# Second home for x of odd groups, batch sums of group 3 on the vector engine, and weight-pair sums two steps ahead

## The reference

```python
# x (32, 64, 512), cond (32, 256)
q_emb = relu(cond @ W3 + b3)
v_sum = sum(x, axis=1, keepdims=True)          # over the 64 tokens of a batch
x1 = (n * x + v_sum) * q_emb[:, None, :]       # n = 64
h0 = relu(x1 @ W2 + b2)
w1, w2 = ternary(W_fc), ternary(W_proj)        # per 64 weights: scale = mean |w|, w -> round(w / scale) in -1, 0, 1, times scale
h = square(relu(h0 @ w1.T))                    # 2048 hidden units
hn = h * rsqrt(mean(square(h)) + eps)
out = x + hn @ w2.T
```

## Time and profile before

| | us |
|---|---|
| median of 3 runs | 320.93 (320.6 to 321.79) |
| the profiled execution | 321.12 |
| its span | 319.1 |
| PE busy | 313.4 (98%), 1326 records |
| DVE busy | 210.6 (66%) |
| ACT busy | 192.1 (60%) |
| POOL busy | 113.0 (35%) |
| granted TensorE clock | 0.998 |

### The profile page before, as it was taken

One profiled execution on the slowest core, in us unless ns is written; L12 is line 12 of the kernel. 1 busy time (PEld: TensorE's weight loads), 2 busy tenths in 40 slices (PEclk: granted clock), 3 DMA queues, 4 the chain that ended last, 5 costly groups with the idle time before them and its releaser, 6 DMA issues.

```text
span 319.1 us, 3835 instructions
## 1 busy us (share of the span) xinstructions
PE 313.4 (98%) x1326; PEld 238.8 (75%) x1326; DVE 210.6 (66%) x290; ACT 192.1 (60%) x282; POOL 113.0 (35%) x94
## 2 busy tenths in 40 slices
PE   8999999999999999999999999999999999999995
PEld 7664746545888788888888888888888888888884
DVE  0539989788888846676556655755655675665555
ACT  1658988799996884455544454644455554445550
POOL 1004333333733535413344431344433314433330
PEclk9999999999999999999999999999999999999999
DMA  6994959489521110016000000600000034000003
GB/s 190 358 279 111 286 138 291 108 191 275 73 49 34 33 36 1 0 46 219 0 0 2 0 0 0 244 23 0 0 2 0 0 116 149 0 0 2 0 1 133
DMA packets 31331, 27.02 MB, mean 85 GB/s; under 512 B 18736, under 2 KB 20816, under 8 KB 31312
## 3 DMA queue, kind: packets, MB, share of 16 engines
q1 hardware_dynamic: 29984, 26.25, 28.9%
q10 hardware_dynamic: 1328, 0.53, 0.7%
HBM read 18.39 MB, written 4.19 MB: 71 GB/s over the span
## 4 chain that ended last, share of the span: by engine, by line
PE 90%; ACT 4%; issue 3%; DVE 2%; POOL 0%; POOLq 0%; DVEq 0%; ACTq 0%
PE ps_out L320 34%; PE ps_acc L308 32%; PE ps_acc L292 17%; PE ps_out L273 5%; ACT x_t L568 1%; ACT x_t L565 1%; PE ps_acc L362 1%; DVE abs_sum L412 1%; DVE y_hi L452 1%; PE ps_x L377 1%; PE ps_acc L369 0%; ACT w_scale L532 0%; ACT w_t L545 0%; ACT w_abs L526 0%; PE ps_x L352 0%
## 5 line engine op out<-in xcount | busy, mean ns | idle before, releaser
L210 POOL TENSOR_TENSOR wv_sb<-wv_sb 128x512 f32<-128x512 f32 x55 | 82.2, 1494 | 114.1 <-ACT wv_sb L571 114.1
L320 PE MATMUL ps_out<-w_t,y_hi 128*128 128x512 f32 x256 | 101.7, 397 | 0.2 <-DVE y_lo L454 0.2
L320 PE MATMUL ps_out<-w_t,y_lo 128*128 128x512 f32 x256 | 101.0, 394 | 0.0
L308 PE MATMUL ps_acc<-h_hi,w_t 128*128 128x512 f32 x256 | 100.1, 391 | 0.0
L308 PE MATMUL ps_acc<-h_lo,w_t 128*128 128x512 f32 x256 | 100.0, 391 | 0.0
L454 DVE TENSOR_TENSOR y_lo<-x_t,y_hi 128x512 fp32r<-128x512 f32 x64 | 91.3, 1427 | 2.2
L565 ACT ACTIVATE x_t<-ps_acc 128x512 f32<-128x512 f32 x64 | 38.1, 595 | 81.1 <-PE ps_acc L308 81.0
L452 DVE CAST y_hi<-x_t 128x512 fp32r<-128x512 f32 x64 | 29.2, 457 | 73.6 <-PE ps_out L320 65.8
L320 PEld LDWEIGHTS ps_out<-w_t,y_hi 128*128 128x128 f32 x256 | 48.1, 188 | 11.5 <-DVE y_lo L454 0.6
L320 PEld LDWEIGHTS ps_out<-w_t,y_lo 128*128 128x128 f32 x256 | 48.4, 189 | 10.9
L308 PEld LDWEIGHTS ps_acc<-h_hi,w_t 128*128 128x128 f32 x256 | 48.3, 189 | 10.6 <-issue 0.2
(11 more groups left out here) (49 smaller groups left out, 147.5 us busy)
## 6 DMA issues: line engine op xcount, KB each, us to landing
...
w_turned<-w_tern SPq DMA_TRANSPOSE x16, 3.1
```

What stands on the lines that cost most here:

```text
L210: engine.tensor_tensor(sq_acc[:], sq_acc[:], y_sq[:, v % SQ_RING, :], ALU.add).then_inc(sq_added, 1)
L308: last = pe.matmul(ps_acc[:, (UNITS + v) % ACC_RING, :], w_t[:, j, k * P:(k + 1) * P], part[:, k, g * BANK:(g + 1) * BANK], start=(k == 0 ...
L320: last = pe.matmul(ps_out[:, t, :], part[:, v % RING, t * P:(t + 1) * P], w, start=(j == 0 and part is y_hi), stop=(j == HJ - 1 and part i ...
```

## The change

It has five parts.

- **A second home for x.** Groups 1 and 3 load into `x_odd`, groups 0 and 2 into `x_sb`. `x_odd` lies where `y_split` (y_hi and y_lo, now one tensor) lies later. `load_x(g)` waits only for the sums of group g - 2, and there is a semaphore for each home. In SP's list, pair 2 now goes ahead of x of group 1, and the loads of groups 2 and 3 stand one turn earlier. The residual's first load waits for 12 counts of `xt_done` instead of 16.
- **Group 3's sums on DVE.** PE only transposes the 16 blocks of group 3 (L293 of after), ahead of unit 8 instead of unit 10. For each k, DVE reduces over the 64 tokens of each batch (L459), forms 64 x + sum (L461) and multiplies with q_t (L466). One k is done at each of the units 8 to 11, where before all four of a group stood at unit 10.
- **Sums one step further ahead.** DVE's step i is now the ternary chain of pair i and then the sum of pair i + 2; sum 1 is done before the loop.
- **ACT's step** spreads the scale of pair i + 1 before it reads pair i + 2.
- **The table of steps**: steps 5, 6 and 10 stand at units 6, 7 and 14, before at 7, 8 and 13.

DVE at units 3 and 4 of the first stage, before. L446 rounds a unit, L412 and L415 sum a pair and make its scales, L422 to L428 are the ternary chain.

```diff
--- before.py
+++ after.py
@@ -77,8 +77,11 @@
 
 
     SUMS_AT = 2
-    STEP_AT_UNIT = {0: 0, 1: 1, 3: 2, 4: 3, 5: 4, 7: 5, 8: 6, 9: 7, 11: 8, 12: 9, 13: 10, 15: 11}
+    STEP_AT_UNIT = {0: 0, 1: 1, 3: 2, 4: 3, 5: 4, 6: 5, 7: 6, 9: 7, 11: 8, 12: 9, 14: 10, 15: 11}
     STEP_AT_TILE = {1: 12, 3: 13, 5: 14, 7: 15}
+    def sums_by_vector(g):
+        return g == GROUPS - 1
+
     KEEP_AT_TILE = {8: 14, 9: 15}
 
     x_rows = x.rearrange("b n d -> (b n) d").rearrange("(g t p) d -> g p t d", p=P, t=TT)
@@ -116,14 +119,20 @@
         w_turned = sb("w_turned", [P, 2 * TT, P], BF16)
         abs_sum = sb("abs_sum", [P, SG], F32)
         scale = sb("scale", [P, RING, SG], BF16)
-        y_hi = sb("y_hi", [P, RING, BANK], F32R)
-        y_lo = sb("y_lo", [P, RING, BANK], F32R)
+
+        with nc.sbuf_tensor("x_odd", [P, TT, D], F32) as x_odd:
+            pass
+        y_split = sb("y_split", [P, 2 * RING, BANK], F32R)
         mean_sq = sb("mean_sq", [P, TT], F32)
         root = sb("root", [P, TT], F32)
         rstd = sb("rstd", [P, TT], F32)
+        batch_sum = sb("batch_sum", [P, GB], F32)
         wq_sb = x1_t[:, 1, 0:KQ, :]
         cond_sb = h0_f[0:BATCHES, 0, 0:Q]
         cond_t = h0_f[:, 1, 0:KQ * BATCHES].rearrange("p (k b) -> p k b", k=KQ)
+        y_hi = y_split[:, 0:RING, :]
+        y_lo = y_split[:, RING:2 * RING, :]
+        x_of = [x_sb[:], x_odd[:]]
         x_res = x_sb
         rstd0 = h0_f[:, 0, 0:TT]
         rsq = h0_f[:, 0, TT:2 * TT]
@@ -150,7 +159,7 @@
         bias_loaded = sem("bias_loaded")
         wv_loaded = [sem(f"wv_loaded{i}") for i in range(KD)]
         x0_loaded = [sem(f"x0_loaded{t}") for t in range(TT)]
-        x_loaded = sem("x_loaded")
+        x_loaded = [sem(f"x_loaded{i}") for i in range(2)]
         res_loaded = sem("res_loaded")
         raw_loaded = [sem(f"raw_loaded{i}") for i in range(RAW_RING)]
         condt_done = sem("condt_done")
@@ -158,6 +167,7 @@
         q_done = sem("q_done")
         q_ready = sem("q_ready")
         xt_done = sem("xt_done")
+        summed = sem("summed")
         x1_ready = sem("x1_ready")
         h0_done = sem("h0_done")
         h0_relued = sem("h0_relued")
@@ -227,12 +237,13 @@
                              ).then_inc(wv_loaded[i], 16)
 
             def load_x(g):
-                sp.wait_ge(xt_done, KD * g)
-                sp.dma_start(x_sb[:], x_rows[g]).then_inc(x_loaded, 16)
+                wait(sp, xt_done, KD * (g - 1))
+                sp.dma_start(x_of[g % 2], x_rows[g]).then_inc(x_loaded[g % 2], 16)
 
             def load_res(g):
                 if g == 0:
-                    sp.wait_ge(xt_done, KD * GROUPS)
+
+                    sp.wait_ge(xt_done, KD * (GROUPS - 1))
                 else:
                     sp.wait_ge(finished, TT * g)
                 sp.dma_start(x_res[:], x_rows[g]).then_inc(res_loaded, 16)
@@ -245,17 +256,17 @@
             load_wv(1)
             load_pair(1)
             load_wv(2)
+            load_pair(2)
             load_x(1)
             load_wv(3)
-            load_pair(2)
             load_pair(3)
             for i in range(len(PAIRS)):
                 if i + RAW_RING + 1 < len(PAIRS):
                     load_pair(i + RAW_RING + 1)
                 turn_pair(i)
-                if i == 1:
+                if i == 0:
                     load_x(2)
-                if i == 4:
+                if i == 3:
                     load_x(3)
                 if i == 9:
                     load_res(0)
@@ -269,16 +280,19 @@
 
         @block.tensor
         def _(pe):
-            def sum_x_block(t, k):
-                return pe.matmul(ps_out[:, k, t * P:(t + 1) * P], x_sb[:, t, k * P:(k + 1) * P], sum_mat[:],
+            def sum_x_block(g, t, k):
+                return pe.matmul(ps_out[:, k, t * P:(t + 1) * P], x_of[g % 2][:, t, k * P:(k + 1) * P], sum_mat[:],
                                  start=True, stop=True)
 
             def sum_x(g):
-                pe.wait_ge(x_loaded, 16 * g)
+                pe.wait_ge(x_loaded[g % 2], 16 * ((g + 1) // 2))
                 pe.wait_ge(x1_ready, KD * g)
                 for k in range(KD):
                     for t in range(TT):
-                        last = sum_x_block(t, k)
+                        if sums_by_vector(g):
+                            last = pe.transpose(ps_out[:, k, t * P:(t + 1) * P], x_of[g % 2][:, t, k * P:(k + 1) * P], ident_f[:])
+                        else:
+                            last = sum_x_block(g, t, k)
                     last.then_inc(xt_done, 1)
 
             def make_h0(u):
@@ -379,13 +393,15 @@
                     last.then_inc(q_done, 1)
                 pe.wait_ge(x0_loaded[t], 16)
                 for k in range(KD):
-                    last = sum_x_block(t, k)
+                    last = sum_x_block(0, t, k)
                     if t == TT - 1:
                         last.then_inc(xt_done, 1)
 
             for u in range(UNITS):
-                if u % KD == SUMS_AT and u // KD + 1 < GROUPS:
+                if u % KD == SUMS_AT and u // KD + 1 < GROUPS - 1:
                     sum_x(u // KD + 1)
+                if u == KD * (GROUPS - 2):
+                    sum_x(GROUPS - 1)
                 make_h0(u)
             for v in range(AHEAD):
                 hidden(v)
@@ -428,15 +444,26 @@
                 dve.tensor_tensor(w_tern[:, i % RING, :], mask, w_scale[:, i % RING, :], ALU.mult).then_inc(tern_ready, 1)
 
             def step(i):
-                if i + 1 < len(PAIRS):
-                    sum_pair(i + 1)
                 ternary_pair(i)
+                if i + 2 < len(PAIRS):
+                    sum_pair(i + 2)
 
             def scale_x(g, k):
                 dve.wait_ge(xt_done, KD * g + k + 1)
                 wait(dve, h0_done, KD * (g - 1))
                 x1 = x1_t[:, g % RING, k, :].rearrange("p (b n) -> p b n", n=N)
-                dve.tensor_tensor(x1, ps_out[:, k, :].rearrange("p (b n) -> p b n", n=N),
+                src = ps_out[:, k, :].rearrange("p (b n) -> p b n", n=N)
+                if sums_by_vector(g):
+                    at = 2 * (KD * [v for v in range(GROUPS) if sums_by_vector(v)].index(g) + k)
+                    wait(dve, summed, at)
+                    dve.tensor_reduce(batch_sum[:], src, AX.X, ALU.add).then_inc(summed, 1)
+                    dve.wait_ge(summed, at + 1)
+                    dve.scalar_tensor_tensor(out=x1, in0=src, scalar=float(N),
+                                             in1=batch_sum[:].rearrange("p (b o) -> p b o", o=1).to_broadcast([P, GB, N]),
+                                             op0=ALU.mult, op1=ALU.add).then_inc(summed, 1)
+                    dve.wait_ge(summed, at + 2)
+                    src = x1
+                dve.tensor_tensor(x1, src,
                                   q_t[:, k, g * GB:(g + 1) * GB].rearrange("p (b o) -> p b o", o=1).to_broadcast([P, GB, N]),
                                   ALU.mult).then_inc(x1_ready, 1)
 
@@ -494,13 +521,16 @@
                 dve.wait_ge(q_ready, k + 1)
                 scale_x(0, k)
             sum_pair(0)
+            sum_pair(1)
             for u in range(UNITS):
                 g, m = u // KD, u % KD
                 if u > 0:
                     round_h0(u - 1)
-                if g + 1 < GROUPS and m == SUMS_AT:
+                if g + 1 < GROUPS - 1 and m == SUMS_AT:
                     for k in range(KD):
                         scale_x(g + 1, k)
+                if g == GROUPS - 2:
+                    scale_x(g + 1, m)
                 if u in STEP_AT_UNIT:
                     step(STEP_AT_UNIT[u])
             round_h0(UNITS - 1)
@@ -548,10 +578,10 @@
             def step(i):
                 if i > 1:
                     keep_pair(i - 2)
+                if i + 1 < len(PAIRS):
+                    spread_pair(i + 1)
                 if i + 2 < len(PAIRS):
                     read_pair(i + 2)
-                if i + 1 < len(PAIRS):
-                    spread_pair(i + 1)
 
             def relu_h0(u):
                 m = u % KD
```

## The result

| | before | after |
|---|---|---|
| median, us | 321.30 (320.60 to 321.79) | 324.41 (324.29 to 325.71) |
| the profiled execution | 321.12 | 324.29 |
| its span | 319.1 | 322.5 |
| DVE busy | 210.6 | 223.6 |
| POOL busy | 113.0 | 116.7 |

The changed kernel is slower: the ratio is 1.0101, with a 95% interval of 1.0077 to 1.0125. The forecast was 325.0, that is 1.013 of the 320.93 it started from; a fourth run of before moved its median to 321.30. One of the ten executions of experiment 3 took 815 us and is outside that experiment's ratio.

The account below looks back on a forecast made before the run. PE bounds the kernel, but DVE's 15.8 us of added work exceeds its 11.8 us of idle time, so y_lo(0) comes at 87.2 instead of PE's 83.1. 320.93 + 4.1 = 325.0 us, forecast 324.3 to 326.2, wider range 320.7 to 327.5.

Parts of the forecast that it names:

- The sum on DVE: DVE's added work before y_lo of tile 0: 1.4 + 5.9 + 8.5 = 15.8 us against 11.8 of idle time.
- (a): DVE before y_lo(0): 14 weight sums lie ahead instead of 13, +1.4 us.
- (b): Group 3's scaling on DVE: four blocks at 2.09 us instead of 0.62, +5.9 us; bounds 1.9 to 2.8 each.
- rival 3: Group 3's new multiply starts before POOL ends and is held, 4 x 0.7 = 2.8 us more, 327.8; chance 0.06.
- (c): First stage: ternary operations right behind a rounding meet POOL's subtraction, +0.99 us in each of seven units, together +8.5.
- PE's saving: Sixteen transposes replace group 3's sum-matrix matmuls on PE: 3.57 us becomes 1.8, saving 1.8 (0 to 2.6).
- PE's stalls: PE stalls some 5.9 us: 2 to 4 before hidden tile 2, 1 to 3 before projection 0.
- Rival 4: PE's clock falls to 1.2 GHz for one unit's work behind a stall, adding 3.4 us, 328.4; chance 0.06.
- The wait before unit 12: PE waits about a microsecond before unit 12 for the last group-3 multiply.
- Loads: DMA and SP: reordered loads put nothing on the path; x for group 1 costs PE 0 to 0.5 us, swallowed later.
- The net: Projection 0 starts at 87.2 instead of 83.1, +4.1 us; PE gives nothing back behind it.
- Rival 1: POOL exclusion costs nothing in the new place; PE keeps its 1.8 us less 0.8: 319.1 to 319.9; chance 0.12.

Follow-up runs that it names:

- experiment 3: Changed kernel with POOL's h0_lo subtraction cut to 8 of 512 columns, h0_lo cleared once at the start: 321.06 us, ratio 0.9980 to before.
- experiment 6: Changed kernel with twelve idle matmuls on PE behind hidden tile 1, to keep the clock up: 323.91 us, ratio 1.0091 to before.
- experiment 7: Kernel before with only the second home of x and its loads added, compute unchanged: 321.31 us, ratio 0.9991 to before.
- experiment 1: Changed kernel with the old order of sums on DVE and ACT's old order, all else kept: 322.29 us, ratio 1.0030 to before.
- experiment 2: Changed kernel with only the rounding moved between ternary chain and sum in eight units: 322.11 us, ratio 1.0023 to before.

## Why the prediction was right, point by point

- **The sum on DVE.** Forecast +15.8 us of work; the groups of instructions in the two stretches, added up, give about 15.0, and without overlaps 14.2. Against it I set 11.8 us of idle time and took 87.2 for y_lo(0)'s end. DVE could fill 10.0, and 86.85 came out, 0.5 of it the late start. So my 86.65, for the case that every gap can be filled, was nearer than the 87.2 that I took.
- **(a) The extra sum** took 1.3 us (forecast 1.4).
- **(b) Group 3's scaling.** Forecast 2.09 us for each block; 53.01 to 55.06 makes 2.05.

```profile
53.01 0.68 DVE L459 TENSOR_REDUCE batch_sum<-ps_out 128x8 f32<-128x512 f32 x1
53.73 0.69 DVE L461 SCALAR_TENSOR_TENSOR x_t<-ps_out,batch_sum 128x512 f32<-128x512 f32 x1
54.45 0.69 DVE L466 TENSOR_TENSOR x_t<-x_t,q_t 128x512 f32<-128x512 f32 x1
55.06 0.42 DVE L473 CAST h_hi<-h_f 128x512 fp32r<-128x512 f32 x1
...
53.17 1.27 POOL L642 TENSOR_TENSOR h_lo<-h_f,h_hi 128x512 fp32r<-128x512 f32 x1 [3.02 <-DVE h_hi L473]
```

  POOL is done at 54.44 and L466 starts at 54.45: rival 3 was out by a hundredth of a microsecond, which is luck as much as foresight. By the rule of the Trainium skill that the prediction cited ("GPSIMD Engine Reference", Key points: contention with two SBUF inputs) L466 was exposed. In no run did this multiply meet POOL (0.69 us in all of them), so whether it would be held isn't shown. On L441 the rule and the trace agree, 1.65 against 0.69 us.
- **(c) The collisions.** All seven units were named rightly, at 1.65 us each (forecast 1.68). (Where the prediction says that "L422's successor" runs from T+0.34 to T+1.02, that is the mask itself, which isn't held.) In unit 14 two operations were held, by 1.08 and 0.95 us (forecast 2.1 together), at y_lo(0) one by 0.96 (forecast 1.0):

```profile
74.34 1.76 DVE L438 TENSOR_TENSOR w_abs<-w_abs,w_scale 128x1024 bf16<-128x1024 bf16 x1
76.13 1.64 DVE L441 TENSOR_TENSOR w_abs<-w_abs,w_sign 128x1024 bf16<-128x1024 bf16 x1
...
74.17 3.06 POOL L642 TENSOR_TENSOR h_lo<-h_f,h_hi 128x512 fp32r<-128x512 f32 x2 [3.02 <-DVE h_hi L473]
```

- **PE's saving.** The sixteen transposes run from 47.04 to 48.78, 1.74 us (forecast 1.8), and the clock stays at 1.00 through them:

```profile
47.04 1.91 PE L293 MATMUL ps_out<-ident_f,x_odd 128*128 128x128 f32 x16
...
47.00:49.00 2.00, 2.00 (x18) 1.94 (x17) 1.97 (x4) 1.73 (x2) 0.50 (x1) 1.00 0.55 195
```

  Of the Trainium skill's rule that transposes don't count as activity ("TensorE: Matmul & The Clock Gate", Part 4: PE-mode transpose) this trace shows no effect.
- **PE's stalls.** Forecast 5.9 us in two parts, 2 to 4 before hidden tile 2 and 1 to 3 before projection 0. The first was 2.62. The second did not show as a wait. Behind the first wait the granted clock fell to 0.50, that is 1.2 GHz, and hidden tile 2 took 3.46 us (83.54 to 87.00) instead of 1.83. The 1.6 us that PE would have waited for y_lo it spent on slow matmuls. Rival 4's mechanism came, but inside the stall, where in this trace it was free (experiment 6). I had counted it as a cost on top.
- **The wait before unit 12.** Forecast about 1 us, measured 0.49:

```profile
65.75 11.43 PE L306 MATMUL ps_acc<-x_t,wv_sb 128*128 128x512 f32 x26 [0.49 <-DVE x_t L466]
```

- **ACT.** It was to wait for the scales of pairs 10 and 12 and did, 3.69 and 1.34 us. But the earlier sums did not remove its waits for a scale, as the prediction also says: between 13 and 88 us they come to 6.1 us, where before had 4.7 in all. That part was wrong, and it cost nothing that the runs show by itself.
- **Loads.** Nothing on the path (experiment 7).
- **The net.** Forecast +4.1 at projection 0, measured 3.9, or 3.4 without the later start. I had said that nothing is given back behind it; there after was 0.5 shorter. The medians of the two kernels differ by 3.1. So the mechanism was right and its size some 0.7 to 1.0 us too large, mostly by the 87.2.
- **Luck.** 324.41 lies 0.1 above the lower end of the forecast's own 324.3 to 326.2. That it lies inside owes something to the base of 320.93: counted from the 321.30 that before took in the end, the range would begin at 324.7, and as a ratio it is 1.0105 to 1.0164, with 1.0101 measured. The wider 320.7 to 327.5 holds either way.

What the prediction didn't see: which relay is next. Rival 1 gave the kernel without collisions 319.1 to 319.9. The experiments with all or nearly all collisions gone (1, 2 and 3) have ratios of 1.0030, 1.0023 and 0.9980, which on the prediction's base of 320.93 is 321.9, 321.7 and 320.3. The term that was too small was the relu of unit 15. I allowed 0.8 us for it; PE waited 1.78 in experiment 1, where the fallen clock took some 0.5 more, and 1.38 in experiment 2 plus 0.84 for y_lo.
